# A four-layer graph network on one core: four PSUM banks for the relation products, a key row written by a transfer, the attribute maximum in another bank, and two scrap tiles for the row maxima

## What is computed

```python
x = layernorm(x + segment_sum(weight_e * (x @ W0)[src], dst) + b0)         # layer 0
# layer 1: two relational convolutions, relu between them
w = einsum('rb,bio->rio', att, basis)              # 2 relations from 30 bases of 512x512
gate = sigmoid(x_j @ gate_w[r])                    # one gate for each node and relation
msg = where(type == 0, (gate0 * x_j) @ w[0], (gate1 * x_j) @ w[1])
agg = segment_sum(msg, row) + x @ root + bias
# layer 2: graph convolution with degree weights
# layer 3: attention over the edges, 8 heads of 64
logits = q[rows] * k[cols] / 8 + attr[edge, head]
p = exp(logits - row_max[rows]); y = segment_sum(p / denom * v[cols]); out = y @ Wo + bo
```

## Time and profile before

| | |
|---|---|
| median of three runs | 1230.68 us (1227.04, 1230.68, 1235.55) |
| profiled execution | 1232.0 us, its span 1230.2 us |
| mean granted TensorE clock | 0.984 of full speed |
| PE busy | 1167.2 us, 95% of the span, 8077 instructions |
| DVE busy | 847.2 us, 69% |
| ACT busy | 442.4 us, 36% |
| POOL busy | 374.1 us, 30% |

### The profile page before, as it was taken

The page is one execution under the profiler, slowest core; times in us unless marked ns, Lnnn a source line. Parts: engine busy times, 40 slices in busy tenths (PEclk is TensorE's granted clock), DMA queues, the critical chain, the costliest instruction groups (busy, mean ns, idle before and its releaser), DMA issues.

```text
span 1230.2 us, 21619 instructions
## 1 busy us (share of the span) xinstructions
PE 1167.2 (95%) x8077; PEld 539.9 (44%) x8078; DVE 847.2 (69%) x1333; ACT 442.4 (36%) x600; POOL 374.1 (30%) x340
## 2 busy tenths in 40 slices
PE   6989999999999989999999999999999899999997
PEld 2334444333444433364444444454333465555553
DVE  7577777344442655652378884657999799899897
ACT  1456666322232222212301103135552355445354
POOL 3034441000350224445554564555557100000000
PEclk9999999999999999999999999999999899999999
DMA  9669995987987988661122212113323566565652
GB/s 311 237 200 326 326 331 150 358 350 261 329 283 272 312 316 286 227 210 2 2 40 47 36 19 70 3 2 45 35 34 58 184 232 228 200 221 198 202 186 111
DMA packets 67490, 222.74 MB, mean 181 GB/s; under 512 B 33200, under 2 KB 38064, under 8 KB 50140
## 3 DMA queue, kind: packets, MB, share of 16 engines
q1 hardware_dynamic: 34846, 156.38, 36.0%
q0 software_dynamic: 28208, 53.10, 18.0%
q10 hardware_dynamic: 4350, 12.07, 2.8%
HBM read 199.90 MB, written 59.92 MB: 211 GB/s over the span
## 4 chain that ended last, share of the span: by engine, by line
PE 45%; DVE 11%; issue 6%; DMA 4%; ACT 2%; ACTq 0%; DVEq 0%
PE PS L1920 13%; PE PS L1872 6%; PE PS L2228 4%; PE PS L2008 4%; PE PS L2215 4%; DVE R L1223 4%; DVE R L1260 4%; DMA w_d<-R 3%; PE PS L2097 2%; PE PS L2274 2%; PE PS L1992 2%; PE PS L1727 2%; PE PS L2245 1%; DVE R L1297 1%; PE PS L1837 1%
## 5 line engine op out<-in xcount | busy, mean ns | idle before, releaser
L844 POOL DMA_INDIRECT bias_d<-R x160 | 276.6, 1729 | 310.2 <-DMA bias_d<-R 204.8
L1920 PE MATMUL PS<-R 128*128 128x512 f16 x900 | 206.3, 382 | 0.0
L810 POOL DMA_DIRECT2D bias_d<-bias_d x159 | 82.6, 526 | 267.3 <-PE PS L1920 123.1
L1683 ACT ACTIVATE R<-PS 128x1024 f32<-128x1024 f32 (+1 forms) x100 | 106.3, 1088 | 108.7 <-PE PS L2215 78.6
L1872 PE MATMUL PS<-W,XX 128*128 128x512 f16 x600 | 137.7, 389 | 5.5 <-DVE R L1042 4.6
L1920 PEld LDWEIGHTS PS<-R 128*128 128x128 f16 x900 | 84.3, 98 | 118.7 <-issue 27.6
L1797 PE MATMUL PS<-R,XX 125*128 125x512 f16 (+2 forms) x612 | 123.1, 343 | 5.7 <-DVE R L958 4.4
L1223 DVE CUSTOM_DVE_ANT_0 R<-PS,R 128x1250 f16<-128x1250 f32 x80 | 116.8, 1460 | 5.5 <-PE PS L2151 2.9
L958 DVE TENSOR_SCALAR R<-W 125x1250 f16<-125x1250 f16 x160 | 89.6, 604 | 37.8 <-PE PS L1797 35.4
L2228 PE MATMUL PS<-R 128*32 128x256 f32 (+1 forms) x1600 | 101.4, 388 | 5.2 <-DVE R L1260 5.2
L2215 PE MATMUL PS<-R 128*128 128x256 f16 (+3 forms) x800 | 100.5, 276 | 5.3 <-ACT R L1683 2.1
(11 more groups left out here) (242 smaller groups left out, 1470.3 us busy)
## 6 DMA issues: line engine op xcount, KB each, us to landing
bias_d<-bias_d POOLq DMA_DIRECT2D x159, 320.0 KB, 5.4
R<-in_basis_s SPq DMA_DIRECT2D x32, 1024.0 KB, 7.2
W<-in_basis_s SPq DMA_DIRECT2D x28, 1024.0 KB, 6.3
W<-bias_d SPq DMA_DIRECT2D x27, 1024.0 KB, 4.9
XX<-bias_d SPq DMA_DIRECT2D x13, 1024.0 KB, 4.9
R<-key_d SPq DMA_DIRECT2D x20, 500.0 KB
R<-R SPq DMA_DIRECT2D x120, 80.0 KB, 4.9
W<-bias_d SPq DMA_DIRECT2D x7, 904.0 KB, 4.6
```

The source lines that it names most:

```text
L844: pool.indirect_dma_start(bias_d, bass.IndirectOffsetOnAxis(ap=idx[:, c:c + 1], axis=0), attr[:, c, :], None, bounds_check=DUMP + GC * P - ...
L1683: S.activation(ER[n % 4][:, :, 0:w, :].rearrange("p g r u -> p g u r"), PS[:, 2 * (n % 2):2 * (n % 2) + 2, :].rearrange("p a (e r) -> p a ...
L1920: ins = T.matmul(mm_out(SUM_BANK(s, i), D), lhs, rhs, start=n == 0, stop=n == len(terms) - 1)
```

## The change

Five things change. The products of s = 1 and s = 2 go round four banks (0, 1, 6, 7; numbers 2 and 3 of s = 1 to banks 4 and 5), and PE waits for the low half of the product four before. The attribute maximum's two small products go into bank 3, beside the gates, and the wait for `bdiff_made` moves from the start of the root products to the first gate of the second convolution; `roots` waits in its place for the products in banks 6 and 7. The row maxima write their sums to `junk` and `junk2` in turn, and DVE waits for its instruction before last. The key row is made by a memset of 128 x 80 elements on POOL, before the scatters, and a transfer on SP, ahead of the head copies; the memset of 1 x 10240 is gone.

```diff
+        junk2 = r1f[:, o1:o1 + NN // 2].bitcast(F16)
...
+        scale_row = r2[:, o2 + NN // 2 + P + DK // 2:o2 + NN // 2 + P + DK // 2 + HEADS * NN // P // 2].bitcast(F16)
...
+        def ZBANK(s, k, r):
+
+            m = k * ZRELS[s] + r
+            if s == 3:
+                return m % 2
+            return 2 + m if s == 1 and m in (2, 3) else (0, 1, 6, 7)[m % 4]
...
+            sp.wait_ge(scale_row_made, 1)
+            sp.wait_ge(loops_out, NT)
+            sp.dma_start(KH[DK:DK + 1, :, :].rearrange("u h (k n) -> u (h k) n", n=HEADS * NN // P),
+                         scale_row).then_inc(kone_made, 16)
             for o_ in range(FT):
                 heads_copied(o_)
...
+            pool.memset(scale_row, MSCALE).then_inc(scale_row_made, 1)
 
             pool.wait_ge(zero_out, 16 * ZF)
             for b in range(BATCHES):
-                if b == BATCHES - 1:
-                    pool.wait_ge(loops_out, NT)
-                    pool.memset(KH[DK:DK + 1, :, :], MSCALE).then_inc(kone_made, 1)
...
                 dve.wait_ge(s_done, idx + 1)
+                if idx >= 2:
+                    dve.wait_ge(s_used, idx - 1)
                 b0 = 3 * (idx % 2)
-                V.tensor_tensor_reduce(out=junk[:, 0:NODES],
+                V.tensor_tensor_reduce(out=(junk, junk2)[idx % 2][:, 0:NODES],
...
-                dve.wait_ge(s_used, idx + 1)
 
             def max_kept(q):
+                dve.wait_ge(s_used, 4 * NT * (q + 1))
...
                 if i == 0 and layer:
                     pe.wait_ge(gate_made, 2)
+                    pe.wait_ge(bdiff_made, 1)
...
-                    if zi >= 2:
-                        pe.wait_ge(zl_made, zi - 1)
+                    held = 2 if s == 3 else 4
+                    if s == 3 or zi - Z0[s] >= held:
+                        pe.wait_ge(zl_made, zi - held + 1)
+                    if (s, k, r) == (1, 3, 0):
+                        pe.wait_ge(xt_made, NT)
+                    if (s, k, r) == (2, 1, 0):
+                        pe.wait_ge(h_made, CHUNKS)
...
-                        ins = T.matmul(mm_out(zi % 2, D), lhs, rhs, start=n == 0, stop=n == len(terms) - 1)
+                        ins = T.matmul(mm_out(ZBANK(s, k, r), D), lhs, rhs, start=n == 0, stop=n == len(terms) - 1)
...
                 if p_:
                     pe.wait_ge(h_made, c - FT + 1)
+                elif f >= 2:
+                    pe.wait_ge(zl_made, Z0[1] + RELS * NT - FT + f + 1)
...
             pe.wait_ge(w16_made, 1)
-            pe.wait_ge(bdiff_made, 1)
             for c in range(FT):
                 roots(c)
...
-            pe.wait_ge(kone_made, 1)
+            pe.wait_ge(kone_made, 16)
```

More of the change, by code:

```diff
@@ L296, in gnn_resnorm @@
         o1 += NT
+        junk2 = r1f[:, o1:o1 + NN // 2].bitcast(F16)
+        assert o1 + NN // 2 <= half
         rden = r1f[:, o1:o1 + QUADS * RB].rearrange("p (q r) -> p q r", q=QUADS)
@@ L302, in gnn_resnorm @@
         negative = r2[0:DK, o2 + NN // 2 + P:o2 + NN // 2 + P + DK // 2].bitcast(F16)
+        scale_row = r2[:, o2 + NN // 2 + P + DK // 2:o2 + NN // 2 + P + DK // 2 + HEADS * NN // P // 2].bitcast(F16)
+        assert o2 + NN // 2 + P + DK // 2 + HEADS * NN // P // 2 <= KEPT
         yT = XX[:, NT * D:NT * D + FT * RB].rearrange("p (f n) -> p f n", f=FT)
@@ L440, in gnn_resnorm @@
         kone_made = sem("kone_made")
+        scale_row_made = sem("scale_row_made")
         wo_in = sem("wo_in")
@@ L1041, in z_low @@
                     scale = dis[:, k:k + 1] if s == 3 else gate[:, k, r:r + 1]
-                    V.scalar_tensor_tensor(Z[:, r, 1, k, :], mm_out(zi % 2, D), scale, Z[:, r, 0, k, :], ALU.mult,
+                    V.scalar_tensor_tensor(Z[:, r, 1, k, :], mm_out(ZBANK(s, k, r), D), scale, Z[:, r, 0, k, :], ALU.mult,
                                            ALU.subtract).then_inc(zl_made, 1)
@@ L1082, in _ @@
                     dve.wait_ge(bmt_done, 1)
-                    step(V.tensor_reduce(bmax1[0:HEADS, :], mm_out(7, EC, HEADS), AX.X, ALU.max))
+                    step(V.tensor_reduce(bmax1[0:HEADS, :], PS[0:HEADS, 3, P:P + EC], AX.X, ALU.max))
                     V.tensor_scalar(diag8[0:HEADS, :], ident[0:HEADS, 0:HEADS], bmax1[0:HEADS, :], None,
@@ L1088, in _ @@
                     V.tensor_tensor(attr[0:EC, :, :], attr[0:EC, :, :],
-                                    PS[0:EC, 6, 0:HEADS].rearrange("p (u h) -> p u h", u=1).broadcast_to(
+                                    PS[0:EC, 3, DK:DK + HEADS].rearrange("p (u h) -> p u h", u=1).broadcast_to(
                                         [EC, CH, HEADS]), ALU.subtract).then_inc(bdiff_made, 1)
@@ L1503, in z_high @@
                     scale = dis[:, k:k + 1] if s == 3 else gate[:, k, r:r + 1]
-                    S.activation(Z[:, r, 0, k, :], mm_out(zi % 2, D), ACT.Copy, scale=scale).then_inc(zh_made, 1)
+                    S.activation(Z[:, r, 0, k, :], mm_out(ZBANK(s, k, r), D), ACT.Copy, scale=scale).then_inc(zh_made, 1)
             for i in range(NT):
@@ L1942, in _ @@
                     pe.wait_ge(bmax_made, 1)
-                    T.transpose(mm_out(7, EC, HEADS), bmax[0:EC, :], ident[0:EC, 0:EC]).then_inc(bmt_done, 1)
+                    T.transpose(PS[0:HEADS, 3, P:P + EC], bmax[0:EC, :], ident[0:EC, 0:EC]).then_inc(bmt_done, 1)
                 if k == 8:
                     pe.wait_ge(bdiag_made, 1)
-                    T.matmul(mm_out(6, HEADS, EC), ones[0:HEADS, 0:EC], diag8[0:HEADS, :], start=True,
+                    T.matmul(PS[0:EC, 3, DK:DK + HEADS], ones[0:HEADS, 0:EC], diag8[0:HEADS, :], start=True,
                              stop=True).then_inc(bmb_done, 1)
```

## The result

The changed kernel takes 1219.82 us, the median of nine runs (1215.44 to 1224.42); the kernel before, on the same chip, 1231.09 (nine runs, 1225.84 to 1240.49). The ratio is 0.990, 95% interval 0.9864 to 0.9935. The forecast was 1216, 14.9 us less than before; the two medians lie 11.3 us apart. The profiled execution took 1216.1 us with a span of 1214.2; that of before 1230.2.

A forecast was written before the change was run, and what follows sets the result against it. No engine binds throughout, so each edit was priced by its own stage's last wait. Terms 4.06 + 4.69 - 0.5 + 3.69 + 0.47 + 2.5 = 14.9 us off 1232.0 gave 1217.1, less 1.3 for the median: 1216 us, range 1209 to 1223.

The forecast's parts named there:

- Products of s = 1: Four banks remove PE's stall at k = 6: 2.28 us idle plus 1.78 of slow clock, gain 4.06 us.
- root products: Moving the subtraction wait removes 3.05 us idle and 1.64 of slow clock ahead of and in them: gain 4.69 us.
- Mixing stage: Second convolution's weight mixing: loads issued 8.75 us earlier meet queued DMA work, giving back 0.5 us (0 to 3.1).
- rival B: Mixing stage takes the DMA queue's time, so all 3.1 us are given back: 1218.4 us, chance 0.17.
- Products of s = 2: Four banks remove stalls at tile 1 (1.87 idle, 1.82 slow clock: 3.69 us) and at k = 6 (0.47 us).
- Row maxima: Dropping DVE's wait after each maximum saves 0.06 us apiece; PE's pace limits the gain to 2.5 us (0 to 4.7).
- The sum: Whole kernel: 4.06 + 4.69 - 0.5 + 3.69 + 0.47 + 2.5 = 14.9 us less, forecast 1216 us.
- Key row: Removing POOL's 8.63 us memset from the scatters gains nothing alone but lets the other gains through.
- A: Row maxima: the wait after each costs nothing, as the next can't start before the READ finishes; 1218.3 us, chance 0.15.
- C: POOL's scatters don't move with PE and end at 954.5, making the maxima's copy 2.7 us late; 1218.5, chance 0.10.
- D: Slower than before: the mixing stage's store landings grow with DMA queue load; 1245.8 us at 5 more each, chance 0.03.
- E: Four banks do nothing, since the data's source delays PE at both places; gain only 6.7 us, 1224, chance 0.04.

The follow-up runs named there:

- e1: Kernel before with only the four banks and the attribute maximum in bank 3; the subtraction wait stays ahead of the root products: 1228.36 us, ratio 0.9991.
- e2: Kernel before, two banks kept, with only the attribute maximum in bank 3 and the subtraction wait moved to the first gate: 1223.51 us, ratio 0.9954.
- e8: Kernel before with a third less PE work for the last three groups' queries and keys and all values, plus two scrap tiles: 1227.92 us, one run.
- e3: Kernel before with only the two scrap tiles and the later wait in the row maxima: 1230.96 us, ratio 1.0028.
- e4: Kernel before with only the key row made by a transfer instead of POOL's memset: 1228.33 us, ratio 0.9979.
- e5: Changed kernel with POOL's memset for the key row put back among the scatters: 1219.64 us, ratio 0.9904.
- e6: Changed kernel with the wait after each row maximum restored and one scrap tile: 1216.43 us, ratio 0.9858.
- e9: The changed kernel measured again, unaltered, beside the kernel before: 1215.96 us, ratio 0.9877.
- e11: Changed kernel with SP's copy of the second half's maxima issued ahead of the loads of `bias_d`: 1218.45 us, ratio 0.9892.
- e7: Kernel before with a third less PE work for the last three groups' queries and keys and all values: 1238.57 us, one run.
- e12: Kernel before with four banks, attribute maximum in bank 3 and key row by a transfer; subtraction wait not moved, one scrap tile: 1222.04 us, ratio 0.9922.
- e10: Same kernel as e6, run again: changed kernel with the wait after each row maximum and one scrap tile: 1216.24 us, ratio 0.9879.

## Why the prediction was right, and where it was not

**Products of s = 1, root products.** 4.06 + 4.69 = 8.75 predicted, 8.8 in the stage's row, and e1 (4.12) and e2 (the 3.05 idle and the slow 1.5 behind it) show the two parts each by itself. Nothing was late in the place of either. Of the 4.06, the 1.78 of slow clock is not sure: in e2 and e8, which keep the two banks, the same stall (2.29) is followed by 48 instructions in 10.52 us.

**Mixing stage.** A give-back of 0.5 (0 to 3.1) was forecast. The two traces show 2.1 gained, but that is the spread of the stage: from the roots' end to the start of s = 2 the kernels with the old start take 154.1 to 156.5 (before, e3, e4), those with the new one 150.8 to 158.7 (the changed one, e1, e2, e5, e6, e9 to e11, mean 154.7 against 155.0). With e7, e8 and e12 too the means are 154.8 and 154.7. So rival B's 3.1 isn't seen, and a give-back of 0.5 is below what these traces tell. Which landings stand in the chain changes from one execution to the next.

**Products of s = 2.** 4.16 predicted, 4.3 found against the profile of before. The idle 1.87 and 0.47 are sure. The 1.82 of slow clock is not: in e3, e4, e7 and e8, which have the same code and the same 1.87 idle, the 24 instructions behind it take 5.34 us. In e3 and e4 the stage takes 289.4, so the banks win 2.6 there. The prediction priced each stall at "its idle time and about as much again"; that is one of two outcomes.

**Row maxima.** The step that was off. The price of the wait is 0.12 us, above the 0.11 that was given as the upper bound, and twice the 0.06 taken; the stage's 2.6 was met (2.5 said) because PE sets its pace in most of it. Group of twenty by group, the stage gave 0.2, 0.5, 0.6 and 1.2, where 0, 0.6, 0.6 and 1.2 were forecast; the last figure came from half of the true price and fits by luck, since PE holds that group too. Of the 2.6 only 1.7 reaches the last value (117.1 us behind the first maximum before, 115.4 now). And the term went into the time as if it were sure to arrive at the end. It arrives only if the last value binds there: not in e3, and e9 against e10 shows none.

**The sum.** 14.9 us were forecast. The two profiled executions differ by 16.0, but that holds 1.8 lost and 2.1 gained in stages that vary so much by themselves; the medians differ by 11.3 in the first measurement and by 15.7 in the second (e9). The 14.9 lies inside the first interval (8 to 17 us), so no term can be called right to a microsecond by the time. That 14.9 and 16.0 lie so near is in part luck.

**Key row.** Worth nothing that can be told alone (e4), and what lets the banks' gain through: 0.9991 against 0.9922 (e1, e12). In the changed kernel its worth isn't shown by the time: e5 was as fast, though its trace has the loads 4.1 us behind the last value. The prediction put the scatters' end at 946.5 and the values' at about 949; 947.2 (944.19 + 3.0) and 947.7 were found.

**The rivals.** A (the wait costs nothing) falls with e7 and e8 as a mechanism, though for the time it comes near. C (the scatters don't move with PE) falls in the profiled execution: the last one starts 15.9 us earlier, of which 8.63 are the memset and 7.1 an earlier start (the first scatter at 404.58, was 411.65). It is half alive: in e10 they are last by 7 us, and in e9 and e11 the last one starts at 948. Its price was mis-sized: the prediction charged 2.7 us for a late copy of the maxima, but what counts is the loads' issue (e11 and the table). Loads at 954.5 instead of some 948 would have cost over 6. D and E don't appear: no landing in the mixing stage's chain of the changed kernel is over 8.1 us, and the idle times went.

## What to carry to other kernels

When a wait has two sources that end within a microsecond of each other, an edit on one of them alone gains little, and edits on both can gain what neither gave; an edit that stands ahead of both, as in e2, gains alone. So find every source of the last wait in a stage before pricing an edit upstream, and test such edits in pairs. Look for the instruction from which the distance to the end is the same in all traces (here a load, not the transfer that PE is seen waiting for), and price each edit by what it does to that one. Set the profiled execution against the median before adding up stages from one trace: e1's trace is 7.2 us shorter than that of before, and its median is the same. Here the next gain has to shorten the scatters and the values at once: behind 530 us POOL's 134 to 137 scatters wait 155 to 161 us for landings of the ones before, in the six kernels read for it, and never for another engine.

## What the runs showed of the hardware that was not expected

**The same stall has two prices.** Behind a stall of the same length and the same code the slow clock comes in some traces and not in others. Behind 2.3 us in the products of s = 1, the 48 instructions take 12.06 to 12.21 us in four traces (before, e3, e4, e7) and 10.52 in two (e2, e8). Behind 3.05 us ahead of the root products, 9.38 to 10.86 in six and 7.96 in one (e1). Behind 1.8 us at the start of s = 2, 7.03 in two (before, e2) and 5.34 in four. The widest pair is e1 and e12. They have the same PE code up to the root products and the same 3.05 us of idle time ahead of them. In e1 the granted clock stays at 1.00 and the 48 instructions take 7.96 us; in e12 it is 0.58 in the window of the stall and 0.74 in the next, the lower of the two levels for part of each, and they take 10.86:

```profile
382.52 7.96 PE L2012 MATMUL PS<-XX,W 128*128 128x384 f16 x48 [3.05 <-DVE R L1100]
```

```profile
381.71 10.86 PE L2014 MATMUL PS<-XX,W 128*128 128x384 f16 x48 [3.05 <-DVE R L1102]
...
380.00:385.00 5.00, 3.29 (x11) 1.64 (x12) 3.61 (x3) 1.96 (x2) 0.00 (x0) 0.58 0.98 378
385.00:390.00 5.00, 5.00 (x25) 2.63 (x24) 0.20 (x1) 0.00 (x0) 0.00 (x0) 0.74 0.99 406
```

What decides between the two stays open.

**A small transfer behind two large ones.** The copy of the maxima lands 2.8 us after its issue when the two 1 MB loads were issued 4.6 to 4.7 us before it (e2, e4), and 6.8 to 6.9 us after when they were issued 0.86 before it (e1, e3, e5). From the chains of e2 and e1:

```profile
959.60 2.79 DMA R<-R
```

```profile
956.65 6.93 DMA R<-R
```

Counted from the first load's issue, it lands after 7.45 to 7.79 us in all seven traces read for it (before, changed, e1 to e5), whenever it was issued itself. In e11 the second load lands 7.4 us behind the first's issue, and the copy, with no load in front, releases PE 2.2 us behind its own. So with the loads in front the copy comes no sooner than they do, which fits with the fixed distance from the loads to PE's restart and to the end.
